# Narrower blocks for the edge-count matrix (128 by 320 in place of 128 by 400), and the step words of three sets in one register load

## The reference, cut to what matters

```
dst = (3125 * uniform(100000) ** 2.0)      # few high numbers, many low ones
src = randint(0, 3125, 100000)
src = concatenate([edge_index[0], arange(N)]);  dst = concatenate([edge_index[1], arange(N)])
out = segment_sum(h[src] * alpha, dst)
```

## Time and profile before

| | |
|---|---|
| median of 3 runs | 3447.66 us (3445.65 to 3448.48) |
| profiled execution: its own time | 3449.33 us |
| its span | 3447.5 us, so 1.8 us lie around it |
| `stage_counts`, first one-hot of DVE to the last clear of ACT | 297.9 to 604.5 us |
| first row of the next stage | 609.44 us |
| PE, DVE, ACT busy over the span | 89%, 77%, 62% |

### The profile page before, as it was taken

The page is one execution under the profiler, slowest core; times in us unless marked ns, Lnnn a source line. Parts: engine busy times, 40 slices in busy tenths (PEclk is TensorE's granted clock), DMA queues, the critical chain, the costliest instruction groups (busy, mean ns, idle before and its releaser), DMA issues. The chain is left out here.

```text
span 3447.5 us, 43195 instructions
## 1 busy us (share of the span) xinstructions
PE 3052.7 (89%) x15721; PEld 1592.6 (46%) x15722; DVE 2646.8 (77%) x2631; ACT 2136.7 (62%) x2651; POOL 248.2 (7%) x379
## 2 busy tenths in 40 slices
PE   3776777898898988899879989999999999979998
PEld 3223333333333334788769853333333333267775
DVE  8998999799999997455442259999999999843433
ACT  3101479799999997111223359999999999834333
POOL 0000000000000000000035400101110101100000
PEclk9998999999999999999989999999999999989998
DMA  2000245677777764544176553333332333210000
GB/s 59 0 0 19 79 164 202 209 234 231 226 232 223 233 222 145 192 149 141 48 202 211 170 202 110 94 92 94 92 94 91 95 92 92 68 67 23 8 8 15
DMA packets 199234, 424.88 MB, mean 123 GB/s; under 512 B 35929, under 2 KB 133457, under 8 KB 199054
## 3 DMA queue, kind: packets, MB, share of 16 engines
q1 hardware_dynamic: 185518, 395.36, 35.8%
q0 software_dynamic: 13536, 27.08, 2.7%
HBM read 354.07 MB, written 61.88 MB: 121 GB/s over the span
## 5 line engine op out<-in xcount | busy, mean ns | idle before, releaser
L1002 PE MATMUL acc<-weights_then_messages,messages 128*64 128x391 f32 x3200 | 571.6, 505 | 81.1 <-DVE weights_then_messages L1067 74.2
L2126 PE MATMUL acc<-weights,keys_and_values 128*64 128x448 f32 x2096 | 451.2, 552 | 2.0 <-DVE weights L2289 1.9
L1002 PEld LDWEIGHTS acc<-weights_then_messages,messages 128*64 128x64 f32 x3200 | 221.3, 139 | 424.9 <-issue 273.2
L2113 PE MATMUL scores<-q,keys_and_values 32*128 32x448 f32 x2800 | 362.6, 587 | 9.5 <-ACT x L2249 4.5
L1064 DVE SCALAR_TENSOR_TENSOR weights_then_messages<-rho,kappa,counts 128x1564 f32<-128x1564 f32 x200 | 367.5, 1837 | 0.0
L1067 DVE TENSOR_TENSOR weights_then_messages<-weights_then_messages,counts 128x1564 f32<-128x1564 f32 x200 | 356.2, 1781 | 11.2 <-ACT weights_then_messages L1025 11.1
L1023 ACT ACTIVATE weights_then_messages<-rho,wx 128x1564 f32<-128x1564 f32 x200 | 317.8, 1589 | 33.2 <-PE acc L1002 31.2
L1025 ACT ACTIVATE weights_then_messages<-weights_then_messages,kappa 128x1564 f32<-128x1564 f32 x200 | 319.9, 1600 | 6.5
L674 PE MATMUL acc<-weights_then_messages 128*128 128x400 bf16 x1024 | 232.3, 359 | 85.3 <-ACT acc L650 44.2
L2286 DVE SCALAR_TENSOR_TENSOR weights<-weights,x 128x3584 f32<-128x3584 f32 x75 | 291.9, 3893 | 4.3 <-DVE weights L2279 1.1
L2251 ACT ACTIVATE weights<-scores 128x896 f32<-128x896 f32 x300 | 287.6, 981 | 10.2 <-PE scores L2113 10.2
(11 more groups left out here) (392 smaller groups left out, 4346.9 us busy)
## 6 DMA issues: line engine op xcount, KB each, us to landing
counts<-edge_counts SPq DMA_DIRECT2D x200, 782.0 KB, 4.5
x<-edge_counts SPq DMA_DIRECT2D x264, 224.0 KB, 2.7
edge_counts<-counts_out SPq DMA_DIRECT2D x40, 1000.0 KB, 4.2
counts<-edge_counts SPq DMA_DIRECT2D x24, 1600.0 KB, 7.9
w_first<-in_L_ffn_W_dram SPq DMA_DIRECT2D x57, 512.0 KB
counts<-edge_counts SPq DMA_DIRECT2D x86, 224.0 KB, 2.7
w_second<-in_L_ffn_W_dram SPq DMA_DIRECT2D x8, 512.0 KB, 8.0
normed_rows<-normed SPq DMA_DIRECT2D x5, 640.0 KB, 4.0
```

The source lines that it names most:

```text
L1002: ins = nc.tensor.matmul(acc[64 * q:64 * q + 64, m, 0:CP], message(t, head(r, q)), w[:, T % WR, q, m * CP:(m + 1) * CP], start=(t == 0), s ...
L2113: ins = nc.tensor.matmul(sc[:, (n + j // 2) % SR, j % 2, 0:CA], kT[part, r % KF, t * P:(t + 1) * P], q[part, r % 2, :], start=True, stop=True)
L2126: ins = nc.tensor.matmul(acc[64 * e:64 * e + 64, p, 0:CA], msg[:, t, r % KF * 2 + p, D * e:D * e + 2 * D], weights(U // 2)[:, 2 * p + e, U ...
```

## The change

CH becomes 320, so that there are 10 columns and 250 blocks, at most 806 + 249 = 1055 steps, and a list of 1056 places, which is 66 sets in place of 64. PE's loop body holds six sets in place of four, and PE loads twelve words at once for three sets in place of four words for each. 1056 steps do not fit two PSUM banks, so `stage_steps` cuts its count and selection matmuls into pieces of 512, 512 and 32 columns in place of two of 512. The division by CH in `stage_front` gets another factor, and the padding target another value. The shared buffer keeps its size (24 * 400 = 9600).

```
-CH = 400
+CH = 320
-STEPS = 1024
+STEPS = 1056
-SETS = 4
+SETS = 6
+LOADED = 3
...
-    H = STEPS // 2
+    PIECES = [slice(a, min(a + 512, STEPS)) for a in range(0, STEPS, 512)]
...
-                    for h in range(2):
-                        ins = nc.tensor.matmul(kps[:, h, 0:H], keys[:, g * P:(g + 1) * P], pick[:, g % 4, h * H:(h + 1) * H],
+                    for piece in PIECES:
+                        ins = nc.tensor.matmul(kps[:, piece], keys[:, g * P:(g + 1) * P], pick[:, g % 4, piece],
                                                start=(g == 0), stop=(g == G - 1))
...
                 with pe.Fori(0, STEPS // SET // SETS) as i:
                     for u in range(SETS):
                         n = SETS * i + u
-                        _, word = nc.values_load_multi_w_load_instructions(
-                            at_step[0:1, bass.ds(n * G, G)], engines=[mybir.EngineType.PE], min_val=0, max_val=(1 << 23) - 1,
-                            skip_runtime_bounds_check_because=IN_TABLE)
+                        if u % LOADED == 0:
+                            _, words = nc.values_load_multi_w_load_instructions(
+                                at_step[0:1, bass.ds(n * G, LOADED * G)], engines=[mybir.EngineType.PE], min_val=0,
+                                max_val=(1 << 23) - 1, skip_runtime_bounds_check_because=IN_TABLE)
+                        word = words[u % LOADED * G:(u % LOADED + 1) * G]
                         pe.wait_ge(s_hs, n + 1)
                         pe.wait_ge(s_hd, n + 1)
```

More of the change, by code:

```diff
@@ L391, in _ @@
                 nc.vector.memset(ids[:, 0, 0:EJ], 0).then_inc(s_pad, 1)
-                nc.vector.memset(ids[:, 1, 0:EJ], 4000).then_inc(s_pad, 1)
+                nc.vector.memset(ids[:, 1, 0:EJ], NP).then_inc(s_pad, 1)
                 nc.vector.memset(X[:, NT - 1, :], 0.0).then_inc(s_xpad, 1)
@@ L406, in _ @@
                 dve.wait_ge(s_ids, 32)
-                link(nc.vector.tensor_scalar(part[:, 0, :], ids[:, 1, :], 2622, None, ALU.mult))
+                link(nc.vector.tensor_scalar(part[:, 0, :], ids[:, 1, :], 3277, None, ALU.mult))
                 link(nc.vector.tensor_scalar(part[:, 1, :], part[:, 0, :], 20, None, ALU.logical_shift_right))
@@ L493, in stage_steps @@
         cut = core.sb(ctx, "cut", [P, 2, STEPS], I32)
-        tps = core.ps(ctx, "tile_counts", [P, 2, 512])
+        tps = core.ps(ctx, "tile_counts", [P, len(PIECES) * 512])
         bps = core.ps(ctx, "block_counts", [P, 512])
-        kps = core.ps(ctx, "step_keys", [P, 2, 512])
+        kps = core.ps(ctx, "step_keys", [P, len(PIECES) * 512])
         s_dve, s_past, s_ended, s_tps, s_bps, s_pick, s_kps = (core.sem(n) for n in (
@@ L503, in _ @@
                     pe.wait_ge(s_past, g + 1)
-                    for h in range(2):
-                        ins = nc.tensor.matmul(tps[:, h, 0:H], ones16[:, :], past[:, g, h * H:(h + 1) * H],
-                                               start=(g == 0), stop=(g == G - 1))
+                    for piece in PIECES:
+                        ins = nc.tensor.matmul(tps[:, piece], ones16[:, :], past[:, g, piece], start=(g == 0), stop=(g == G - 1))
                 ins.then_inc(s_tps, 1)
@@ L533, in _ @@
                 dve.wait_ge(s_tps, 1)
-                link(nc.vector.tensor_copy(tnow[:, :].rearrange("p (h n) -> p h n", h=2), tps[:, :, 0:H]))
+                link(nc.vector.tensor_copy(tnow[:, :], tps[:, 0:STEPS]))
                 def pick_tile(g):
@@ L566, in _ @@
                 link(nc.vector.scalar_tensor_tensor(
-                    out=rel[:, :].rearrange("p (h n) -> p h n", h=2), in0=block_of[:, :].rearrange("p (h n) -> p h n", h=2),
-                    scalar=-65536.0, in1=kps[:, :, 0:H], op0=ALU.mult, op1=ALU.add))
+                    out=rel[:, :], in0=block_of[:, :], scalar=-65536.0, in1=kps[:, 0:STEPS], op0=ALU.mult, op1=ALU.add))
                 link(nc.vector.tensor_scalar(cut[:, 0, :], rel[:, :], 7, None, ALU.arith_shift_right))
@@ L1104, in __init__ @@
         self.wdb = core.sb(ctx, "w_dst_columns", [P, KF, 1, P])
-        place = core.sb(ctx, "weights_then_messages", [P, 24 * CH])
+        place = core.sb(ctx, "weights_then_messages", [P, 9600])
         self.place = place
```

## The result

| | before | after |
|---|---|---|
| median of 5 runs | 3447.66 us (3439.50 to 3452.09) | 3464.38 us (3461.34 to 3470.23) |
| profiled execution, its own time | 3449.33 us | 3470.14 us |
| its span | 3447.5 us | 3468.3 us |

The ratio after to before is 1.0054, with a 95% interval of 1.0038 to 1.0070: slower, by 16.7 us. The forecast was 3443.9 in a range of 3432 to 3456, so it was wrong, and its likeliest case (the same within 6.9 us) too. The two profiled executions stand 20.8 us apart.

The account below looks back on a forecast made before the run. DVE was taken to bound the count stage's first half, ACT the second; after, the ring binds the first. Count stage -5.8, tail -0.9, step stage +2.9 sum to -3.8: 3443.9 us by the median, range 3432 to 3456.

Parts of the forecast that it names:

- likeliest case: Whole kernel: a time within 6.9 us of before, which the measurement cannot tell from no change; chance 0.42.
- the ring: Count stage, first half: DVE and PE alternate over two one-hot buffers; after the change this binds at 3.99 us a set.
- The border between the halves: Count stage: dst 1600 parts DVE's first half (203.1 us before) from ACT's second (103.5 us before).
- The rival in which the ring does not bind: First half: matmuls shrink in proportion to columns, DVE's 3.87 us a set rules, -13.5 us, kernel 3430.4; chance 0.12.
- the register load: PE's gaps between sets: twelve words take some 0.52 us, and the long gap overruns by 0.30 in every third set.
- The rival "the twelve-word load does not do what it says": PE's load is split or priced by the word; slower from 0.74 us more a load on; chance 0.07.
- the clock: Rival, first half: TensorE stays at 1.2 GHz, +0.45 us a set, +19.4 if all are cold, kernel 3463; chance 0.08.
- 189.8: Forecast first half of the count stage in us, 13.3 less than 203.1, with 3.5 for lag and low clock.
- Second half: Count stage, ACT's copies and clears: 125 blocks in place of 100 at 0.89 us each, 111.0 us, +7.5.
- The step stage: Third pieces of 32 columns in the count and selection matmuls: +2.9 us, 1.9 of it for f32 selection matmuls.
- my additions of 0.3 and 0.8: Step stage: 0.3 us for each group's third weight load, 0.8 for bf16 pieces with wider DVE operations.
- The tail: Last clear to next stage: the last set becomes real work and the stage closes with the last store, -0.9 us.

Follow-up runs that it names:

- e5: The changed kernel with three buffers of both one-hots in place of two, twelve-word loads kept: 3446.07 us, 0.9996 of before.
- e4: The kernel before (400 columns) with sixteen words for four sets in one load: 3470.13 us, 1.0062 of before.
- e1: The changed kernel with one load of four words per set again: 3455.23 us, 1.0021 of before.
- e2: The changed kernel with four matmuls of zeros behind each set, twelve-word loads kept: 3456.16 us, 1.0021 of before.
- e3: The changed kernel with one four-word load per set and four matmuls of zeros behind each set: 3456.52 us, 1.0023 of before.
- e6: The changed kernel with three buffers of one-hots and one four-word load per set: 3457.01 us, 1.0022 of before.
- e9: The changed kernel with three buffers of one-hots and eight words for two sets per load: 3446.03 us, 1.0001 of before.
- e8: The changed kernel with eight words for two sets per load, two buffers kept: 3448.23 us, 1.0001 of before.
- e7: The kernel before (400 columns) with four matmuls of zeros behind each set: 3444.73 us, 0.9990 of before.

## Why the prediction was wrong

**The bound and the ring: right.** The border between the halves, the cheaper `hot_d` (0.67 us less, 2.82), the ring's parts (0.48, 0.13, 3.96, and 3.43 where I gave 3.41 for 16 matmuls: 8.00 for two sets, of 7.98) and its taking the bound from DVE all show in the profile. e5 shows the ring's part by adding a buffer to it. The rival in which the ring does not bind fell with it.

**The step that failed: the register load.** I priced a word from two rows, one word on ACT (0.266) and four words on PE (0.334), and drew a line through them: 23 ns a word, 0.52 us for twelve. The medians or quick values that the runs show are 0.334 for four words, 0.59 for eight, 0.85 for twelve and 1.10 for sixteen: 65 ns for each word beyond the fourth. One word and four cost nearly the same, and they came from two engines; a line through two such points says nothing of its slope further out. I also wrote that the extra of a slow load "is no matter of words", as it was some 0.62 for one word and for four. It grows: the longest loads took 0.97, 1.84, 2.35 and 2.80 us for four, eight, twelve and sixteen words. And I took one in six to be slow, where 5 of 14 were, with 5.4 us over the quick ones together.

When a load is slow stands in the traces: when a store of finished blocks is on its way. Two slow loads (384.85, 452.49) and two quick ones, as stretches of the changed kernel; the last two numbers are the busy share of the DMA engines and their GB/s:

```profile
384.85:386.60 1.75, 0.00 (x0) 0.00 (x0) 1.75 (x2) 0.00 (x0) 0.00 (x0) 0.83 0.90 325
399.51:400.36 0.85, 0.19 (x2) 0.00 (x0) 0.68 (x2) 0.60 (x2) 0.00 (x0) 1.00 0.00 0
425.34:426.19 0.85, 0.19 (x2) 0.00 (x0) 0.68 (x2) 0.82 (x3) 0.00 (x0) 1.00 0.00 0
452.49:454.48 1.99, 0.80 (x3) 0.15 (x1) 1.18 (x2) 1.29 (x4) 0.00 (x0) 0.50 0.95 340
```

A store of 800 KB keeps the DMA engines moving for 2.4 us. From the first one-hot on, all 8 slow loads of this trace have such a store under them, and 1 of the 13 quick ones, by less than 0.1 us. Over the 14 traces it is each of the 195 loads that took a quarter more than the shortest, and 49 of the 346 others. So a longer load meets a store more often, and more of its words meet it. The forecast put ACT's slow loads to the stores, and left PE's out of that. No run changed the stores alone.

In the terms of the prediction: the gap with a quick load overran the ring by 0.70 in place of 0.30, +5.8 over 14.5 loads, and the slow ones cost 5.4 in place of 1.3, +4.1. That is 9.9 us on the first half, or 0.68 a load. The rival "the twelve-word load does not do what it says" had this mechanism and a deciding point of 0.74 a load; the load came to within 0.06 of it, and its chance of 0.07 was too small. The Trainium skill's rate of about 200 ns per register ("Runtime: NRT & Kernel Launch", section "Instruction fetch mechanics"; it speaks of loads from HBM) would by my estimate be 2.4 us for twelve words. The median here does not agree (0.86), and the slowest load comes near it (2.35).

**The second one: the clock.** I argued that the clock rose for good at 350, and gave its staying low 0.08. But I had assumed for it that PE keeps working as it did, only with fewer columns. The long loads made it rest instead, in most gaps for 1.1 to 3.1 us between sets of 3.4, and the clock fell again and again, for 97 us; a long load at 400 columns (e4) and the short one at 320 (e1) show that it was mostly the load and not the columns. What that cost is the difference of e2 to after in the first half: 208.3 - 200.7 = 7.6. With it the sum is 189.8 + 9.9 + 7.6 = 207.3, of 208.3 measured, and without it 199.7, of e2's 200.7. That both come so close is in part luck, since 189.8 has 3.5 us in it for lag and low clock, which no run took apart. The two terms are not independent. Where the loads are short the same zeros give nothing (e3 to e1: 0.5), as there little low clock is left to take away (25 us in e1's first half, counted from the first one-hot, and 80 in that of after). So I had two slower rivals, both thought unlikely and each worked out alone, and one mechanism set off both.

**Second half: 111.0 forecast, 114.7 measured.** The mechanism was right: the copy takes 0.42 and the clear 0.43, the period is 0.82 in the median, and with loads of four words, or eight in three buffers, this half is 111.0 to 111.2 (e1, e6, e9). The rest of 3.7 goes with the load of twelve words: six of the 124 periods are over 1.3 us, in e1 none, and the clock explains only 1.1 of it (e2).

**The step stage: +2.9 forecast, +0.9 measured.** The selection matmuls went from 14.00 to 15.71 us, which is 1.7 for 16 records, 0.107 each, close to the lower row that I had taken (1.9 in all). From that stage to the first one-hot the loss is 1.5, so my additions of 0.3 and 0.8 were too much; the front was 0.65 us shorter.

```profile
269.73 15.71 PE L515 MATMUL step_keys<-weights_then_messages,keys 128*128 128x512 f32 x48 [1.28 <-DVE weights_then_messages L538]
```

**The tail: right, and its cost overlooked.** The stage closes 1.1 us sooner after the last clear. I counted the last set of left-over places as waste. But it kept PE at work up to the border: the next stage's 32 matmuls in f32 started 0.32 us after PE's last one and took 10.75 us. After the change PE rests 7.08 us before them, and they take 13.77. The granted clock over them is 1.00 before and 0.78 after, that is 6.1 us at half speed, which is just the 3.0 us. First before, then after:

```profile
609.47 10.75 PE L829 MATMUL row<-xt,w_dst_columns 128*128 128x391 f32 x32 [0.32 <-PEq L605]
```
```profile
625.68 13.77 PE L830 MATMUL row<-xt,w_dst_columns 128*128 128x391 f32 x32 [7.08 <-PEq L604]
```

In every kernel of 400 columns that stage gets to its first L1002 / L1003 matmul 18.7 us after these start, and in every one of 320 columns after 20.1 to 21.7. So the narrow blocks gain 1.1 there and lose 1.4 to 3.0. This I had at nothing. No run gave PE work in that pause, so that the lost set is the cause is read from the rows and not tested.

**What stays open.** 1.6 us of the difference lie behind that point, and I found no place for them; the same remainder moves by more than that between kernels that differ in the count stage alone. e5, e8 and e9 reach the next stage some 3 us earlier than the kernel before (606.5 to 607.0 against 609.5) and end no earlier: in part that is the start of that stage, and in part their profiled executions, which took 3.2 to 7.7 us more than the medians; the rest is not settled.

## What to carry to other kernels

A price per element from two small instances is no price for a large one: where an edit merges several register loads, measure the merged one, its slow instances too, and set it against the slack of the chain that it stands in, not against the time that the calls saved. Merging costs even where the sum of the loads falls (here from 33.0 to 27.0 us from the first one-hot on), since what counts is the longest pause that the buffers can take in; size the batch to the ring, or the ring to the batch. And before you drop work that looks like waste at a stage's end, see whether TensorE's clock in the next stage hangs on it.

## What the runs showed of the hardware that was not expected

- A register load on PE from SBUF takes 0.33, 0.59, 0.85 and 1.10 us for 4, 8, 12 and 16 words when quick, and up to 0.97, 1.84, 2.35 and 2.80 us when slow; 8 of 22 loads of twelve words were slow. Every slow load, on PE (195 of 195 in the 14 traces) and on ACT, fell together with a store of finished blocks to DRAM.
- The granted clock fell back to 1.2 GHz in a stage in which PE was busy three quarters of the time (113 of 150 us; the kernel before, busy 115, stayed at 2.4), with pauses mostly of 1.1 to 3.1 us between runs of 3.4 us; four matmuls of zeros behind each set brought it from 0.84 to 0.98 at no cost that can be seen (e2), and at 400 columns from 0.83 to 1.00 ahead of 350 us (e7).
- 16 matmuls of 320 columns take 3.43 us and 16 of 400 take 3.51: a fifth fewer columns buy 2%, in this loop, where the bank comes from a register.
